# Fetching the active experts' rows by register-addressed DMA instead of by selection matmuls, and reordering one vector slot

## The reference, cut to what matters

```
# layer 0: gated input, then an FFN with 8-bit activations and ternary weights
g  = sigmoid(conv5(mean of x over the first length[b] columns))  # per row of x
h0 = x * g
x1 = x + down(silu(gate(q(h0))) * up(q(h0)))       # 1376 hidden columns, gate/up/down ternary, q = 8-bit rounding by row maximum
# layer 1: a codebook-quantised linear map, then base product plus 4 active experts of 16
xc = x1 @ w_eff.T                                   # w_eff from cond_weight, codebook and a rank-64 product
y  = xc @ W_base.T + b_base
A, Bm = lora_A[active], lora_B[active]              # (4, 8, 512) and (4, 512, 8)
logits = (xc @ router_W.T + router_b)[..., active]
alpha  = softmax(log(domain_prior[active] + 1e-12) + logits)
out = x1 + y + sum_e alpha_e * ((xc @ A_e.T) @ Bm_e.T) * 2
```

## Time and profile before

| | us |
|---|---|
| median of 3 runs | 153.8 (153.78 to 153.96) |
| profiled execution, its own time | 153.92 |
| its span, first to last instruction | 152.1 |
| PE busy | 138.4 |
| DVE busy | 114.1 |
| ACT busy | 96.1 |
| POOL busy | 11.0 |

### The profile page before, as it was taken

The page is one execution under the profiler, slowest core; times in us unless marked ns, Lnnn a source line. Parts: engine busy times, 40 slices in busy tenths (PEclk is TensorE's granted clock), DMA queues, the critical chain, the costliest instruction groups (busy, mean ns, idle before and its releaser), DMA issues.

```text
span 152.1 us, 2134 instructions
## 1 busy us (share of the span) xinstructions
PE 138.4 (91%) x661; PEld 84.7 (56%) x661; DVE 114.1 (75%) x302; ACT 96.1 (63%) x156; POOL 11.0 (7%) x31
## 2 busy tenths in 40 slices
PE   6779999998799967898579999999999999999993
PEld 2256665753356544446234545454576766797792
DVE  2799999989999999999978856998996031035561
ACT  3799998996997975965365659797663403400200
POOL 7000000000000033200004200000000000000000
PEclk9999999999999999999968999999999999999999
DMA  5999999849600430603100905150400000000193
GB/s 172 336 402 421 419 414 404 323 130 396 225 0 0 86 45 5 129 0 69 26 0 0 166 2 107 22 97 2 95 0 4 0 0 0 4 0 0 63 377 112
DMA packets 19486, 19.22 MB, mean 126 GB/s; under 512 B 13474, under 2 KB 13858, under 8 KB 19476
## 3 DMA queue, kind: packets, MB, share of 16 engines
q1 hardware_dynamic: 19476, 19.10, 39.8%
HBM read 13.82 MB, written 2.10 MB: 105 GB/s over the span
## 4 chain that ended last, share of the span: by engine, by line
PE 50%; DVE 27%; ACT 10%; issue 8%; DMA 2%; SPq 0%; ACTq 0%; DVEq 0%
PE bank L971 15%; PE bank L918 12%; ACT tern_d L526 6%; PE bank L881 6%; PE bank L887 6%; DVE hmax L1322 5%; DVE raw_gate L1319 4%; PE bank L929 3%; DVE junk L1158 2%; DMA cond<-in_cond_w 2%; DVE rmax L1208 2%; ACT cond L492 2%; PE bank L978 1%; DVE tern_i L1203 1%; PE bank L863 1%
## 5 line engine op out<-in xcount | busy, mean ns | idle before, releaser
L881 PE MATMUL bank<-tern_g,head_sb 128*128 128x464 bf16 (+1 forms) x96 | 22.6, 357 | 1.0 <-DVE tern_u L1204 0.8
L887 PE MATMUL bank<-tern_u,head_sb 128*128 128x464 bf16 (+1 forms) x96 | 22.5, 357 | 0.6 <-DVE raw_gate L1319 0.6
L918 PE MATMUL bank<-tern_d,delta 128*128 128x512 bf16 (+1 forms) x88 | 22.0, 399 | 0.5 <-DVE tern_d L1204 0.5
L971 PE MATMUL bank<-m_h,fr 128*128 128x512 f32 (+1 forms) x72 | 22.3, 378 | 0.0
L1319 DVE TENSOR_TENSOR raw_gate<-bank,wbt 128x464 f32<-128x464 f32 (+1 forms) x24 | 15.1, 631 | 4.2 <-ACT wbt L624 3.7
L624 ACT ACTIVATE wbt<-bank,s_g 128x464 f32<-128x464 f32 (+1 forms) x24 | 14.9, 633 | 3.4 <-PE bank L881 3.3
L1322 DVE TENSOR_REDUCE hmax<-raw_gate 128x1 f32<-128x464 f32 (+1 forms) x24 | 15.1, 631 | 0.8
L631 ACT ACTIVATE raw_gate<-raw_gate,hq 128x1376 int16<-128x1376 f32 x8 | 11.5, 1438 | 6.5 <-DVE hq L1329 6.5
L918 PEld LDWEIGHTS bank<-tern_d,delta 128*128 128x128 bf16 (+1 forms) x88 | 9.0, 103 | 11.5 <-issue 1.9
L887 PEld LDWEIGHTS bank<-tern_u,head_sb 128*128 128x128 bf16 x96 | 9.3, 98 | 10.0 <-DVE raw_gate L1319 1.2
L796 PE MATMUL bank<-wbt,cond 128*128 128x512 f32 x32 | 14.8, 599 | 0.0
(11 more groups left out here) (177 smaller groups left out, 226.8 us busy)
## 6 DMA issues: line engine op xcount, KB each, us to landing
raw_gate<-in_w_gate_t SPq DMA_DIRECT2D x4, 688.0 KB, 7.4
raw_up<-in_w_up_t SPq DMA_DIRECT2D x4, 688.0 KB, 12.3
xs<-in_x SPq DMA_DIRECT2D x8, 256.0 KB, 13.2
out_x<-xs SPq DMA_DIRECT2D x7, 256.0 KB, 2.2
raw_down<-in_w_down_t SPq DMA_DIRECT2D x2, 768.0 KB, 5.4
cond<-in_cond_w SPq DMA_DIRECT2D x4, 256.0 KB, 4.6
wbt<-in_w_base_t SPq DMA_DIRECT2D x4, 256.0 KB, 9.2
raw_down<-in_w_down_t SPq DMA_DIRECT2D x2, 512.0 KB, 7.6
```

What stands on the lines that cost most here:

```text
L881: mm = pe.matmul(bank_g[n % 2][:, 0:w], xq_t[:, b % 2, k, :], tern_g[:, k, f0:f0 + w], start=(k == 0), stop=(k == KH - 1))
L887: mm = pe.matmul(bank_u[n % 2][:, 0:w], xq_t[:, b % 2, k, :], tern_u[:, k, f0:f0 + w], start=(k == 0), stop=(k == KH - 1))
L918: mm = pe.matmul(bank_down[:], h_t[0:rows, b % 2, j, :], tern_d[0:rows, j, :], start=(j == 0), stop=(j == KF - 1))
L971: pe.matmul(bank_y[n_res][:, h0:h1], a[:, b, k, :], m[:, k, h0:h1], start=(n == 0), stop=False)
```

## The change

- The 4 expert indices are made whole and clamped in `lengths()` (two operations that stood in `selectors()`, and a copy to integers). SP reads them into registers and issues, with those registers in the source address, 8 small DMAs for the A and router rows (after the down weights' loads) and 16 for the B rows and the priors (in its loop, after `transpose_x(4)`). `lora1` is laid out by expert. The loads of all of lora1 (512 KB) and of the router (32 KB) are gone.
- `selectors()`, the copy of the priors, POOL's iota for them, `selection`, `b_rows` and one PSUM copy are gone; PE transposes the 36 fetched rows (`selected_rows`) in slot 1.
- ACT's scaling of the B rows moves from slot 2 to slot 5. The logarithm of the priors moves from ACT's early part to the start of the tail, behind a table load of its own. `log_prior` moves into DVE's tail.
- `weight_sum_down(3)` and `(4)` move from DVE to ACT, in slot 1 behind `x_evacuate(2)`.
- The maximum over a row's chunk maxima (`hred`) is folded into the last chunk's maximum: the chunk maxima now lie behind the row's hidden values.
- `normalise(k)` waits for each of ACT's four activations by itself, not for the last of them.
- Slot 3 on DVE: `x_max(5, 8)` stood ahead of `residual(0)`. Now `x_max(5, 6)` and `x_max(6, 7)` stand at the end of slot 2 and `x_max(7, 8)` behind `y_safe(2)`; `ms_l` stands right behind `residual(0)`, ahead of `hidden_chunk(3, 1)`.

```diff
@@ sync
-            sp.dma_start(rwp[:], router).then_inc(ld_router, 16)
...
-            sp.dma_start(l1ab[:], lora1).then_inc(ld_exp, 16)
-            sp.dma_start(b_full[3 * ZC:ZS, :], b_base).then_inc(ld_exp, 16)
+            sp.dma_start(b_full[3 * ZC:ZS, :], b_base).then_inc(ld_base, 16)
...
+            def load_rows(a):
+                sp.dma_start(sel_rows[a * RK:(a + 1) * RK, :],
+                             lora1[bass.ds(expert[a], 1), :, 0, :].rearrange("o r h -> (o r) h"))\
+                    .then_inc(ld_sel_rows, 16)
+                sp.dma_start(sel_rows[ZC + a:ZC + a + 1, :], router[bass.ds(expert[a], 1), 0:H])\
+                    .then_inc(ld_sel_rows, 16)
+
+            def load_b(a):
+                for i in range(3):
+                    sp.dma_start(b_full[i * ZC + a * RK:i * ZC + (a + 1) * RK, :],
+                                 lora1[bass.ds(expert[a], 1), :, 1, :].rearrange("o r h -> (o r) h"))\
+                        .then_inc(ld_sel_b, 16)
+                sp.dma_start(pr_sel[:, a, :], router[bass.ds(expert[a], 1), H:H + 2].broadcast_to([P, 2]))\
+                    .then_inc(ld_sel_prior, 16)
...
+            sp.wait_ge(act_done, 1)
+            expert = [sp.value_load(act_idx[0:1, a:a + 1], min_val=0, max_val=NE - 1) for a in range(NACT)]
+            for a in range(NACT):
+                load_rows(a)
...
+                if b == 1:
+                    for a in range(NACT):
+                        load_b(a)
@@ scalar
-                    ins = act.activation(cond[:, k, c], cond[:, k, c], ACT.Copy, scale=scl_inv[:, k, g:g + 1])
-                ins.then_inc(condn_done, 1)
+                    act.activation(cond[:, k, c], cond[:, k, c], ACT.Copy,
+                                   scale=scl_inv[:, k, g:g + 1]).then_inc(condn_done, 1)
...
-                    act.activation(pr[:, 0:1], pr[:, 0:1], ACT.Ln, bias=eps12[0:NE, 0:1]).then_inc(lp_done, 1)
...
+                if b == 1:
+                    weight_sum_down(3)
+                    weight_sum_down(4)
...
-                if b == 2:
-                    act.wait_ge(b_ps, 1)
+                if b == 5:
+                    act.wait_ge(ld_sel_b, 16 * 3 * NACT)
...
+            act.preload_act_table_set("natural_log_exp_and_others")
+            act.wait_ge(ld_sel_prior, 16 * NACT)
+            act.wait_ge(eps_done, 3)
+            act.activation(ln_prior[:], pr_sel[:, :, 0], ACT.Ln, bias=eps12[:, 0:1]).then_inc(lp_done, 1)
@@ tensor
+            def selected_rows():
+                pe.wait_ge(ld_sel_rows, 16 * 2 * NACT)
+                pe.wait_ge(ident_done, 2)
+                pe.wait_ge(mfull_done, KH)
+                for k in range(KH):
+                    mm = pe.transpose(bank_sel[:, k * ZL:(k + 1) * ZL], sel_rows[:, k * P:(k + 1) * P],
+                                      ident[0:ZL, 0:ZL])
+                mm.then_inc(sel_ps, 1)
...
             def down(b):
                 if b == 0:
-                    pe.wait_ge(b_full_done, 1)
+                    pe.wait_ge(wtot_read, 3)
@@ vector
-            def selectors():
                 link(dve.tensor_tensor(act_f[:], act_f[:], act_n[:], ALU.add))
                 link(dve.tensor_scalar(act_f[:], act_f[:], 0.0, float(NE - 1), ALU.max, ALU.min))
...
+                dve.tensor_copy(act_idx[:], act_f[:]).then_inc(act_done, 1)
...
-                link(dve.tensor_reduce(hmax[:, b % 2, c:c + 1], hs, AX.X, ALU.max, apply_absolute_value=True))
+                if c < NC - 1:
+                    row_max, src = hrow[b % 2][:, F + c:F + c + 1], hs
+                else:
+                    row_max, src = hred[:, b:b + 1], hrow[b % 2][:, f0:F + NC - 1]
+                link(dve.tensor_reduce(row_max, src, AX.X, ALU.max, apply_absolute_value=True))
...
-                link(dve.tensor_reduce(hred[:, o], hmax[:, b % 2, :], AX.X, ALU.max))
...
                 if b == 3:
-                    x_max(5, NB)
                     residual(0)
+                    dve.wait_ge(msh_done, 1)
+                    dve.tensor_tensor(ms_l, bank_ms.rearrange("p (k c) -> p k c", k=KH),
+                                      ms_h.bitcast(F32), ALU.subtract).then_inc(msl_done, 1)
...
                     y_safe(2)
-                if b == 1:
-                    weight_sum_down(3)
-                    weight_sum_down(4)
+                    x_max(7, NB)
...
                     y_mean(2)
+                    x_max(5, 6)
+                    x_max(6, 7)
...
             dve.wait_ge(ml_done, KH)
+            dve.wait_ge(lp_done, 1)
+            link(dve.tensor_tensor(log_prior[:], ln_prior[:], pr_sel[:, :, 1], ALU.add))
```

More of the change, by code:

```diff
@@ L180, in build @@
         act_n = sb("act_n", [P, NACT])
[L181 to L184, removed]
+        act_idx = sb("act_idx", [P, NACT], I32)
+        pr_sel = sb("pr_sel", [P, NACT, 2])
+        ln_prior = sb("ln_prior", [P, NACT])
         log_prior = sb("log_prior", [P, NACT])
@@ L224, in build @@
         silu = wbt_flat[:, 0:2 * CHUNKS[0][1]].rearrange("p (i f) -> p i f", i=2)
-        hbuf = [raw[0][:, i * F:(i + 1) * F] for i in range(2)]
-        patterns = raw[0][:, 2 * F:4 * F].bitcast(I16)
+        hrow = [raw[0][:, i * (F + NC - 1):(i + 1) * (F + NC - 1)] for i in range(2)]
+        hbuf = [row[:, 0:F] for row in hrow]
+        patterns = raw[0][:, 2 * F + 8:4 * F].bitcast(I16)
         h_i = patterns[:, 0:2 * KF * P].rearrange("p (i f) -> p i f", i=2)
-        h_bits = raw[0][:, 2 * F:4 * F].bitcast(BF16)[:, 0:2 * KF * P].rearrange("p (i f) -> p i f", i=2)
+        h_bits = raw[0][:, 2 * F + 8:4 * F].bitcast(BF16)[:, 0:2 * KF * P].rearrange("p (i f) -> p i f", i=2)
         ht_i = patterns[:, 2 * KF * P:3 * KF * P].rearrange("p (j e) -> p j e", j=KF)
         xt_i = patterns[:, 3 * KF * P:3 * KF * P + 2 * H].rearrange("p (i k e) -> p i k e", i=2, k=KH)
-        hmax = sb("hmax", [P, 2, NC])
         hred = sb("hred", [P, NB])
@@ L747, in weight_total @@
                 else:
-                    pe.wait_ge(wsum_done[i], SUMMED_BY_ACT)
-                    pe.wait_ge(dsum_dve_done, parts - SUMMED_BY_ACT)
+                    pe.wait_ge(wsum_done[i], parts)
                 if i == 0:
                     pe.wait_ge(delta_done, KH)
-                    pe.wait_ge(iota_done, 5)
+                    pe.wait_ge(iota_done, 4)
                 elif i == 1:
@@ L757, in weight_total @@
                 pe.matmul(dst, ones[:], wsum[:, i, 0:parts], start=True, stop=True).then_inc(wtot_ps, 1)
[L759 to L766, removed]
-                    pe.matmul(bank_sel[:, k * ZL:k * ZL + ZC], l1a[:, k * P:(k + 1) * P], sel_er[:, 0:ZC],
-                              start=True, stop=True)
-                    pe.matmul(bank_sel[:, k * ZL + ZC:(k + 1) * ZL], rw[:, k * P:(k + 1) * P], sel_e[:],
-                              start=True, stop=True)
-                else:
-                    for i in range(2):
-                        mm = pe.matmul(bank_sel[:, KH * ZL + i * NACT:KH * ZL + (i + 1) * NACT], pr_bc[:, i, :],
-                                       sel_e[:], start=True, stop=True)
-                    mm.then_inc(sel_ps, 1)
+            def selected_rows():
[6 more added lines that the diff above has]
+                mm.then_inc(sel_ps, 1)
             def codebook(k):
@@ L799, in fold @@
                     mm.then_inc(fold_ps, 1)
-            def b_rows():
-                pe.wait_ge(wtot_read, 3)
-                pe.wait_ge(sel_done, 2)
-                pe.wait_ge(ld_exp, 32)
-                pe.matmul(bank_b[0:3 * ZC, :], sel_er[:], l1b, start=True, stop=True).then_inc(b_ps, 1)
             def conv(g):
@@ L1004, in _ @@
                 if b == 1:
[L1005 to L1006 removed]
+                    selected_rows()
                 if b == 2:
@@ L1297, in stacked_b @@
                                          ALU.mult, ALU.add).then_inc(b_done, 1)
-                link(dve.tensor_tensor(log_prior[:], lg[:, 0, :], lg[:, 1, :], ALU.add))
             def ternary_down(i):
@@ L1303, in ternary_down @@
                         rows, rounded_by_act=2 * NC + 1 + DOWN_BY_ACT.index(i) if i in DOWN_BY_ACT else 0)
-            def weight_sum_down(i):
-                j0, n, rows = DOWN_PARTS[i]
-                dve.wait_ge(ld_down[i], 16)
-                dve.tensor_reduce(wsum[0:rows, 2, i:i + 1], raw_down[0:rows, j0:j0 + n, :].rearrange("p j h -> p (j h)"),
-                                  AX.X, ALU.add, apply_absolute_value=True).then_inc(dsum_dve_done, 1)
             def hidden_chunk(b, c):
```

56 lines of the change are left out of this document (10 added, 46 removed).

## The result

The changed kernel takes 152.13 us (median of 20 runs, 150.96 to 153.03) where the kernel before took 153.81 (153.18 to 155.21). The ratio is 0.988, with a 95% interval of 0.986 to 0.991: 1.8 us less, where the prediction had 3.3 less. The profiled execution is one of the fastest of these runs (151.12 us, the fourth of the 20), with a span of 149.3. Against the 153.92 and 152.1 of before that is 2.8 us less. So there are two things to explain: why the profiled execution gained 2.8 and not 3.3, and why the median gained a further 1.0 less. The profiled time lies inside the forecast's own range of 149.9 to 151.3, the median above it.

The account below looks back on a forecast made before the run. DVE's chain before 77 us was taken to set the start of a PE-bound part. `x1_transposes(0)` 3.2 us earlier plus 1.87 of slow clock made 5.1, of which `residual(1)` lets 3.3 through: 153.92 - 3.3 = 150.6 us, range 149.9 to 151.3.

Parts of the forecast that it names:

- The hinge: First `x1_transposes(0)` in slot 3, released by DVE's `ms_l`, where the PE-bound part starts: from 77.02 to 73.8 us.
- The start: Separate activation waits in `normalise`, against extra small instructions in `lengths()` and an ended wait in `y_safe(0)`: -0.1 us in sum.
- the selectors: Slot 0 on DVE: 1.19 us of instructions go, `y_safe(1)` moves from 46.24 to 45.86, DVE then waits 0.9 us for ACT.
- the sums: Parts 3 and 4 moved to ACT in slot 1: `weight_scale(2)` at 57.1 us, `hidden_chunk(2, 0)` at 60.05, not 61.54.
- The hand-over to `residual(1)`: Slot 3: `residual(1)` ends at 81.4 us, not 83.04, and PE waits for it, so 3.3 of 5.1 us comes through.
- The bound of 0.70: SP's sixteen `load_b` copies are covered up to 0.70 us each; above that every 0.1 us costs 1.6 us.
- The tail: At the kernel's end, the table load (1.28 us) and logarithm (0.28) cost nothing, with 1.8 us of cover.
- From there PE runs without a gap as before: After the second transposes at 81.4 us: `x_evacuate(5)` (84.3 us) is ready before `gate_up(5, 0)` (85.9).
- I take it that the clock stays up: Around `x1_transposes(0)` in slot 3: PE idles 0.7 us, not 2.6, so the 1.87 us cost of the slow clock goes.
- the first rival: The low clock moves to slot 1, adding 1.2 us after ACT's slack: 151.8 us; chance 0.15.
- the second rival: ACT keeps more of what DVE gives, so the sums' 1.3 us becomes 0.3: 151.6 to 152.5 us; chance 0.10.
- SP is late: SP's copy issues take 0.70 us or more: gain shrinks (150.6 to 153.8) or kernel slower (156.8 at 1.12); chance 0.25.

Follow-up runs that it names:

- Experiment 6: Changed kernel with ACT's `silu_chunk(5, 0)` ahead of `hidden_evacuate(3)` and `hidden_round(4)`: 151.92 us, 0.988 of the kernel before.
- experiment 1: Kernel before with only DVE's new order of slot 3: 153.10 us, ratio 0.995.
- experiment 3: Changed kernel with the sums of parts 3 and 4 back on DVE: 152.89 us, 0.993 of the kernel before.
- experiment 4: Kernel before with the register-addressed row fetch alone, all other edits undone: 153.31 us, ratio 0.994.
- experiment 8: Kernel before with 10 matmuls on zeros ahead of `x1_transposes(0)` to hold the clock: 153.20 us, ratio 0.996.
- experiment 11: Changed kernel with slot 3's old DVE order and the clock held by 12 plus 8 matmuls on zeros: 151.50 us, 0.985 of the kernel before.
- experiment 9: Changed kernel with the clock held and, on SP, `transpose_h(3)` ahead of `transpose_x(5)`: 152.22 us, 0.990 of the kernel before.
- experiment 12: Kernel before with the row fetch alone and the clock held at three places by 22 matmuls on zeros: 153.11 us, ratio 0.996.

## Why the prediction was right in its sign and 1.5 us too low

**What held.** The hinge and what releases it: `ms_l` done at 73.58, `x1_transposes(0)` at 74.34 and, with the clock held, at 73.71, where 73.8 was predicted. The start (0.13 us where 0.1 was said), the selectors (45.92 where 45.86 was said, and the wait for ACT that comes then), the sums (57.17 where 57.1 was said; 60.15 where 60.05 was), each within 0.1 us. The hand-over to `residual(1)`, by which most of the 1.87 us of the slow clock does not count: it ends at 80.94 where 81.4 was predicted, 0.4 us better. SP: 0.44 us for each copy, with 0.6 taken. The bound of 0.70 was too generous: the copies began at 63.64 and not 62.5, and ACT was ready at 76.5 and not 77.3, which makes it (76.5 - 3.6 - 63.6) / 16 = 0.58. The tail: the table load and the logarithm cost nothing, as all from the second transposes on is the old time plus slot 5's gap (149.3 - 81.00 = 68.3 against 152.1 - 84.68 = 67.4).

**First step that failed: "From there PE runs without a gap as before".** The prediction looked at `x_evacuate(5)` as the only thing that could be late for slot 5. What ran late was `silu_chunk(5, 0)`, behind `hidden_evacuate(3)` in ACT's order, which waits for a transposition that SP issues behind `transpose_x(5)`; and the chain that feeds that one (DVE, POOL, SP) got 2.1 us earlier while PE got 3.7. PE loses 0.80 us there. Experiment 6, which lets the activation go first, takes the gap out of the trace (8.43 to 7.46 us between two transposes), though 0.3 us of it comes back one slot later, and experiment 1 shows the gap without the fetch. The prediction had "PE gaps after 82 us" among its signs of being wrong, and this is one. The sum was: 150.6 + 0.9 for what stands behind 81.00 us - 0.4 for the earlier `residual(1)` = 151.1, the time of the profiled execution (151.12). The two errors have opposite signs, so the forecast for it looks better than its parts.

**Second step that failed: "I take it that the clock stays up".** In the profiled execution it fell at 70 us, where it cost nothing at the end. In others it costs more: the median of 20 runs is 1.0 us above the kernel with the clock held, 151.12. The drop in slot 1 was the first rival, at 0.15, and its price of 1.2 us is what experiment 6's trace shows (82.23 less 81.00). Whether the slower runs of the changed kernel have their drop just there is not shown, since none of them has a trace; it is seen in slot 1 in the traces of experiments 3, 4, 6 and 8. 151.1 + 1.0 = 152.1 is the median; the 1.0 is the measured difference of two medians, not worked out from where the clock falls. The forecast was a case without either cost and it treated the rival as an alternative. In fact the clock of one kernel falls in different places from one execution to the next, and the median takes in all of them. That the median also lies in the range of the second rival (151.6 to 152.5) is chance: the sums were done on ACT as counted.

**The parts.** The prediction gave the fetch nothing of PE's and 0.4 us for DVE's selectors; alone it gives 0.8 (0.994, 0.991 to 0.997). The order at the hinge it put at 1.7 us (0.4 + 1.3), and 1.6 to 1.8 was found there (experiments 1 and 11). Of that 0.4 to 0.6 reaches the end in the changed kernel, and about 0.8 in the kernel before, where the order also takes away the low clock behind the hinge. The sums bring 0.8 to 1.0; the prediction's own steps give 0.9 (1.5 at `hidden_chunk(2, 0)`, less the 0.6 it had before).

**The rivals.** "SP is late" was given 0.25 and is out: the row of b_base, 1.12 us, was the price of the backlog and not of copies with few rows; the same load takes 0.33 us at 15.62 us in the changed kernel. "ACT keeps more" did not come: the sums were done as counted. On the rule of the Trainium skill (DMA: Bandwidth & Descriptors, why a DMA increments its semaphore by 16): a copy of eight rows took SP 0.28 to 0.36 us by the trace, less than the 0.46 of one with 128 rows. So if the sequencer does write the rest of the 16 itself, that did not make these copies dearer to issue than one of 128 rows. No two runs differ by the extra write alone, so its own time stays unknown.

## What to carry to other kernels

When an edit moves the bound engine's start earlier, follow each of its next few waits to the end of its own chain, through DMA queues and the other engines' orders: a wait that was hidden while the engine itself was late shows up when the engine gains more (3.7 us here) than the chain behind the wait does (2.1). A price at the hinge is only worth what the next hurdle lets through; find that hurdle first. Where a kernel's idle gaps on TensorE are near those behind which the clock fell in any trace, hold the clock with matmuls on zeros in the idle time and time that version too, or forecast a mean over the places where the clock can fall and not the best case.

## What the runs showed of the hardware that I had not expected

- A copy with a register in its address is cheap to issue: 0.28 us for 8 rows and 0.23 for one (0.36 for the very first), 0.44 from one to the next with the register work between, and 0.36 for the priors spread over 128 partitions.
- A transposition by DMA that is issued right behind another can land late, but need not. Slot 3's h behind x took 5.2 us in the kernel before, 4.76 in the changed kernel, 4.2 in experiment 6 and 3.6, the median, in experiment 8. Slot 3's x behind h took 4.3 us in experiment 9, but x's right behind h's in slots 1 and 4 of the same run took 2.7. What decides it was not tried.
- The granted clock falls in different places in different executions of one kernel, with means from 0.966 to 0.989 in 20 runs and 2 us between the fastest and the slowest. Twelve matmuls on zeros, in time that PE would have idled, raised the mean to 1.00, with a spread of 0.7 us in six runs. In experiment 12, 22 of them held it in only six runs of twelve.
